# A two-attention, two-expert layer on one core: the gradient products of the second attention alternate between the upper and the lower half of the array

## The reference

```python
def step(carry, inp):
    w0_, w1_, w2_ = carry
    qi, ki, vi, lr0i, lr1i, lr2i = inp
    gate = ki @ w0_
    hb = ki @ w2_
    sg = silu(gate)
    hidden = sg * hb
    dhidden = vi @ w1_.transpose(0, 2, 1)
    dhbm = dhidden * sg
    dgate = dhidden * hb
    dgba = silu_backprop(dgate, gate)
    w1g = newtonschulz5(jnp.einsum('bch,bcd->bhd', hidden * lr1i, vi))
    w0g = newtonschulz5(jnp.einsum('bcd,bch->bdh', ki * lr0i, dgba))
    w2g = newtonschulz5(jnp.einsum('bcd,bch->bdh', ki * lr2i, dhbm))
    ...   # w += wg, each column scaled back to its first norm
    oi = silu(qi @ w0_) * (qi @ w2_) @ w1_
    return ((w0_, w1_, w2_), oi)
```

## Time and profile before

| | |
|---|---|
| median of 3 runs | 1790.38 us (1789.67 to 1796.13) |
| span of the profiled execution | 1800.7 us (no other time of it is given) |
| second attention, steady part | 1438.4 to 1710.0 us |
| one period in it | 20.54 us; 22.06 us in four periods that also project outputs |
| busy over the span | PE 95%, DVE 83%, ACT 67%, POOL 61% |
| mean granted clock of TensorE | 0.979 |

### The profile page before, as it was taken

How to read it: one execution, slowest core, us unless ns; L and a number is a source line. 1 busy time by engine, 2 the same in 40 slices (tenths; PEclk the granted TensorE clock), 3 DMA queues, 4 the chain that set the end, 5 groups by cost and what they waited for, 6 DMA issues and landing times.

```text
span 1800.7 us, 41462 instructions
## 1 busy us (share of the span) xinstructions
PE 1710.1 (95%) x14070; PEld 1245.5 (69%) x14070; DVE 1490.8 (83%) x3492; ACT 1202.2 (67%) x2911; POOL 1104.9 (61%) x1148
## 2 busy tenths in 40 slices
PE   7999899999999999999999999999998788888888
PEld 5577567777777777777777777777766566666667
DVE  5322599999999999999999999999986788888863
ACT  2134477777777777777777777777754488778863
POOL 1600067777777777766666666666676477778841
PEclk9999999999999999999999999999987699999999
DMA  9423300100110110100000000001001000000032
GB/s 310 148 92 109 104 31 22 37 30 26 30 38 24 33 35 21 38 18 27 24 18 24 29 12 29 23 18 29 15 1 60 1 1 1 2 1 1 1 88 90
DMA packets 66096, 73.83 MB, mean 41 GB/s; under 512 B 10975, under 2 KB 54767, under 8 KB 65775
## 3 DMA queue, kind: packets, MB, share of 16 engines
q1 hardware_dynamic: 62919, 63.92, 11.7%
q0 software_dynamic: 3072, 8.65, 1.4%
HBM read 55.45 MB, written 17.10 MB: 40 GB/s over the span
## 4 chain that ended last, share of the span: by engine, by line
PE 80%; DVE 9%; ACT 5%; POOL 3%; issue 2%; DMA 1%; SPq 0%; POOLq 0%; DVEq 0%; ACTq 0%
PE banks L735 19%; PE banks L893 6%; PE banks L762 4%; PE banks L770 3%; PE banks L849 3%; PE banks L868 3%; PE banks L778 3%; PE banks L807 3%; PE banks L821 3%; PE banks L700 3%; PE banks L815 2%; PE banks L949 2%; PE banks L814 2%; PE banks L1025 2%; PE banks L719 2%
## 5 line engine op out<-in xcount | busy, mean ns | idle before, releaser
L735 PE MATMUL banks<-xnT,hw 128*128 128x512 f32 x768 | 414.1, 622 | 2.5 <-DVE cv L2034 2.5
L2088 DVE CAST_PREDICATED MM<-lmask,banks 128x512 bf16<-128x512 uint32 x384 | 272.2, 709 | 36.6 <-PE banks L815 32.5
L2034 DVE SCALAR_TENSOR_TENSOR cv<-banks,hc,cv 128x510 f32<-128x510 f32 (+2 forms) x384 | 284.0, 740 | 5.9 <-ACT cv L1439 1.2
L1503 ACT ACTIVATE T<-banks 128x256 bf16<-128x256 f32 x384 | 149.7, 390 | 147.0 <-PE banks L807 146.4
L2692 POOL TENSOR_TENSOR X<-X,yrow 128x512 f32<-128x512 f32 x128 | 163.2, 1275 | 66.5 <-ACT yrow L1535 66.5
L2656 POOL TENSOR_TENSOR kn<-nsum,half_pos 128x4 f32<-128x4 f32 x64 | 65.6, 1025 | 143.3 <-DVE nsum L2059 143.3
L815 PEld LDWEIGHTS banks<-MM,T 128*128 128x128 bf16 x1536 | 104.3, 98 | 65.3 <-issue 48.3
L814 PEld LDWEIGHTS banks<-T,MM 128*128 128x128 bf16 x1280 | 99.2, 97 | 65.4 <-ACT T L1503 63.2
L807 PEld LDWEIGHTS banks<-MM,Gb 128*128 128x128 bf16 x1536 | 79.4, 98 | 93.6 <-DVE MM L2088 53.7
L893 PE MATMUL banks<-ho,OT 128*128 128x256 f32 x512 | 143.0, 403 | 0.0
L2034 DVE SCALAR_TENSOR_TENSOR cv<-banks,hcv,cv 128x510 f32<-128x510 f32 (+2 forms) x192 | 141.4, 736 | 1.4 <-ACT cv L1439 1.3
(11 more groups left out here) (318 smaller groups left out, 4902.7 us busy)
## 6 DMA issues: line engine op xcount, KB each, us to landing
MM<-in_eye SPq DMA_DIRECT2D x64, 256.0 KB, 2.6
slot_rows<-zeros SPq DMA_DIRECT2D x1, 5304.0 KB, 20.6
xs<-slot_rows SPq DMA_DIRECT2D x13, 408.0 KB, 3.9
slot_out<-ye SPq DMA_DIRECT2D x13, 384.0 KB, 2.7
hw<-in_hw SPq DMA_DIRECT2D x16, 256.0 KB, 3.3
wT<-in_winit SPq DMA_DIRECT2D x8, 384.0 KB, 3.8
wgu<-in_wgu SPq DMA_DIRECT2D x1, 2816.0 KB
w1c<-in_ew SPq DMA_DIRECT2D x16, 176.0 KB
```

The costliest lines, as they stand in the source:

```text
L735: ins = pe.matmul(PROJ[t][:], hw[:, kk, t, :], xnT[:, kk, u.b * BLK:(u.b + 1) * BLK], start=(kk == 0), stop=(kk == KD - 1))
L1503: act.activation(strips(T1[:].rearrange("p i t -> p (i t)"), LEVELS[lv], 0, 1), grams_bank(u)[:, 0:TILES * 64].rearrange("p (k e) -> p k e ...
L2034: dve.scalar_tensor_tensor(o, y, taps_of(t)[:, TAPS - 1 - i:TAPS - i], o, ALU.mult, ALU.add).then_inc(dve_conv, 1)
L2088: dve.copy_predicated(dst, m, ps).then_inc(dve_mm, 1)
```

## The change

The loop over the halves `b` becomes the innermost of the three loops in `grads`.

```diff
                 else:
                     pe.wait_ge(t_gk, 3 * u.n + 1)
                     pe.wait_ge(t_hlr, 2 * u.n + 2)
-                for b in range(2):
-                    rows = slice(b * CH, (b + 1) * CH)
-                    for n, m in enumerate(((0, 1), (2,))[s]):
-                        for h in range(H1):
+                for n, m in enumerate(((0, 1), (2,))[s]):
+                    for h in range(H1):
+                        for b in range(2):
+                            rows = slice(b * CH, (b + 1) * CH)
                             r = RB[u.p][rows, m, h, :] if m < 2 else vv[u.p][rows, h, :]
                             last = pe.matmul(bank[2 * u.p + b][:, (2 * n + h) * P:(2 * n + h + 1) * P], LA[u.p][rows, m, h, :], r,
                                              start=True, stop=True)
```

## The result

The changed kernel takes **1798.4 us** (median; 1792.7 at least) where the kernel before, timed beside it on the same chip, takes 1796.5 us. The ratio is 1.0032, with a 95% interval of 1.0018 to 1.0047: it is slower by about 5.7 us, and 1782.6 us (0.44% less) was forecast. The medians lie only 1.9 us apart because the runs of either kernel fall into two groups, 1787 to 1790 and 1796 to 1798 us before, 1793 to 1796 and 1801 to 1805 after; each group has moved up by about 6. Three executions that took far longer are left out of the ratios: 9178 us of the changed kernel, 9480 of experiment 3 and 2753 of the kernel before. The profiled execution spans 1801.7 us (its own time 1803.5), that of before 1800.7.

A forecast was written before the change was run, and what follows sets the result against it. It took one chain alternating between engines, with the first `grads` call on it, to bound the period; 7.6 + 0.2 = 7.8 us off 1790.4 gave 1782.6 us, own range 1780.5 to 1784.5, 8-in-10 range 1779.5 to 1789.5.

The forecast's parts named there:

- steps 1 and 2: The two `grads` calls: the first falls from 1.711 to 1.170 us, 0.54 less; the second stays at 0.72.
- Rivals B: First call: only neighbouring records of different halves overlap, so it takes 1.37 us; gain 4.8 us, about 1785.6; chance 7%.
- C: Both calls: each change of half drains, first call 2.76 us; slower, 1805 up to 1815 us; chance 5%.
- step 3: Work behind the first call: all waits are in time, L2295 with 0.02 us to spare, so all 0.54 us passes.
- The condition written at the end: Sign of error: call shortens, period does not; then idle time before L2295 is gone and another releaser stands there.
- The chain that held 1.64 us of L1014: Chain of waits over one period of the second attention: all of the first call, 1.64 us, lies on it.
- step 4: Pairs 2 to 15 at full clock: 14 first calls gain 0.54 us each, 7.6 us in all.
- step 5: Pairs 0 and 1, lower clock: gain between 0 and 2.0 us; 0.2 taken for pair 0, 0 for pair 1.
- rival D: Pairs 0 and 1 give most of 2.0 us, or lower-clock stretches shorten: 1779 to 1781.4 us; chance 8%.
- Rival A: Gain absorbed by a wait, or late start has another cause: 1790 us (1789 to 1791); chance 12%.

The follow-up runs named there:

- experiment 3: The changed kernel with TensorE turning weight 0 twice (duplicate work before L1021): 1789.3 us, ratio 0.998 to the kernel before.
- experiment 2: The kernel before (old order) with DVE's L2230 moved one place later, behind L2264: 1791.0 us, ratio 0.9976 to the kernel before.
- experiments 1: The changed kernel with DVE's L2230 moved one place later, behind L2264: 1783.0 us, ratio 0.9926 to the kernel before.
- 4: The changed kernel with POOL's L2780 scaling one of its two weights only: 1778.5 us, ratio 0.9909 to the kernel before.
- experiment 8: The changed kernel itself, timed again beside the kernel before: 1795.3 us, ratio 1.0027.
- 9: The changed kernel with weight 0 turned twice, timed again: 1791.6 us, ratio 0.9994 to the kernel before.
- 10: The kernel before (old order) with weight 0 turned twice: 1796.9 us, ratio 1.0017 to the kernel before.
- 6: The kernel before with the new order for pairs 8 to 11 alone: 1804.4 us, ratio 1.0015 to the kernel before.
- experiment 7: The kernel before with its order made matrix, half, row of heads (four records of one half, then four of the other): one profiled run, 1804.5 us.

## Why the prediction was wrong

- **The call (steps 1 and 2): right.** 1.16 for 1.17 us, 0.72 unchanged, two records in flight. Rivals B and C fall with it: all 14 calls of the steady part took 1.16, not 1.37 or over 1.71 us.
- **"So all of 0.54 passes" (step 3): this step failed.** Its parts on L2295, L1613 and L2764 came true (L2295 1.97 us after the call, 1.98 forecast). But it asked of each engine only whether its next waiting row would be in time, and took it that "all that comes after hangs on PE or DVE and moves along". It said of POOL that it "stands idle for 1.82 us before its next step, L2764, so it has more room than 0.54". POOL did have room; what had none was DVE's L2230 behind POOL's L2780, which stood 0.50 us long in the kernel before, against 0.16 free, and was passed over as DVE work. With the call 0.54 us shorter it stood 1.05 us long, and the period stayed at 20.54. The condition written at the end, that the period stays though the call shortens, is what happened: the idle time before L2295 is gone. But no new releaser is named anywhere, since the stall is inside L2230.
- **The chain that held 1.64 us of L1014** The earlier trace rows was read as proof that the call sets the period. It was one of two paths, and the shorter one (20.24 against 20.54, experiment 2): the chain follows rows, and a hold inside a row is no edge in it. The chain of the kernel before did hold the sign, L2230 with 0.42 us where it has 0.08 when free (experiments 1 and 2 have that in their chains); the prediction does not show that row.
- **How often (step 4):** 14 × 0.54 = 7.6 came to 0.95. Only the period from pair 2 to pair 3 shortened, 20.54 to 19.59, the one in which L2230 is not held.
- **The lower clock (allowance in step 5 and rival D): mis-sized.** ± 1.5 us was allowed, in the lead-in. In the steady part the falls cost 1.68 + 1.67 + 1.68 + 1.42 = 6.5 us in the profiled execution; in one of them PE L1102 takes 3.14 us for 1.89. At the experts' start the lower level lasts 6.8 us instead of 3.4, and the end lies 0.6 us later.
- **Rival A** had the mechanism's first half (absorbed, 12%) but not what followed, so it gave 1790 us and no loss. No rival had a lower clock as a result of the shorter call.

The difference between the two profiled executions, added up: the first call of pair 0 starts 1.26 us earlier (ahead of the change), from there to pair 2 it is 3.9 less, the first period 0.95 less, the falls 6.5 more, the end 0.6 more: +1.0, as the spans have it. The 3.9 are not the change's: over the profiled executions that stretch takes 51.6 to 56.7 us in the old order and 50.7 to 56.3 in the new, 54.1 and 52.9 in the mean. With 1.2 for it instead, the sum is -1.2 - 0.95 + 6.5 + 0.6 = +4.9, near the 5.7 measured; the 1.2 is itself unsure, with a spread of 5 us, and this execution need not be a typical one.

**Settled:** the hold sets the period (1, 2 and 4), and the loss is the lower clock that comes with less PE work (8 against 9 and 10 by the mean clocks of 12 runs each; the traces, 3 included, agree, but are one execution each). **Open:** why falls stand in four periods of one execution, in two of another and in none of 6 and 7, and only at pairs 8 to 11; and why single runs of one kernel differ by some 8 us at one mean clock (1788 and 1797 in the kernel before), which lies partly ahead of the second attention, where pair 0 starts anywhere from 1371.8 to 1388.8 us.

## What to carry to other kernels

Before an engine's time is taken off a chain, compare the length of each small row beside another engine's row with the same form elsewhere: one that is too long and ends with its neighbour is a wait that no view lists as one, and it may close a second ring around the work that gets faster. If that ring is as long as the period, mend it first: here one place in an order was worth 0.30 us a pair in the old order of the products and 0.84 in the new, since only then did the shortening pay in full. Where the period does not shrink, a faster TensorE only idles more, and its clock can fall, as it did here: the saving then costs time.

## What the runs showed of the hardware

- TensorE can start records of one half of the array ahead of waiting records of the other half that were issued before them: with eight records of the other half ahead, the second stream starts some 0.55 us late (an estimate from the earlier trace rows; the call takes 1.71 us); with four (1.26 us, experiment 7) or two (1.16 us) ahead two records fly at the start.
- A DVE TENSOR_SCALAR of 0.16 us took 0.50, 0.95 and 1.05 us where it came second to a POOL TENSOR_TENSOR of 1.04 us, and 0.16 where it started 0.05 us ahead of one, while a TENSOR_REDUCE beside POOL took its 1.21.
- With PE busy 19.59 of 22.06 us the granted clock stayed at the upper level; with 19.04 it stayed in some periods and fell to 0.50 for 3.4 us in others, 1.2 to 1.9 us behind the wait of 1.36 us before L1021 (the kernel after and experiment 8); with 19.47 (duplicate work) it stayed, and so it did with 19.04 of 21.22.
